# A gated delta-rule layer with expert routing on one core: later convolutions behind each inverse, and the inverse's first blocks stored and loaded first

## The reference

```
x = hidden_states                                   # (1, 2048, 512)
h = layernorm(x)
q, k, v = (silu(conv4(h @ W)) for W in (Wq, Wk, Wv))   # causal convolution over 4 tokens, per column
q, k = l2norm(q), l2norm(k);  beta = sigmoid(h @ Wb)
for each token t:                                   # per head, state S is 64 x 64
    u = beta * (v - k @ S);  S = S + outer(k, u);  o = (q / 8) @ S
x = x + (rmsnorm(o) * norm_w) @ Wo
```

## Time and profile before

| | us |
|---|---|
| median of 3 runs (lowest, highest) | 1327.56 (1323.68, 1330.0) |
| the profiled execution | 1325.61 |
| its span, first to last instruction | 1323.6 |
| PE busy | 1274.0 |
| DVE busy | 865.5 |
| ACT busy | 373.7 |
| POOL busy | 338.3 |
| mean granted TensorE clock | 0.988 |

### The profile page before, as it was taken

One profiled execution on the slowest core, in us unless ns is written; L12 is line 12 of the kernel. 1 busy time (PEld: TensorE's weight loads), 2 busy tenths in 40 slices (PEclk: granted clock), 3 DMA queues, 4 the chain that ended last, 5 costly groups with the idle time before them and its releaser, 6 DMA issues.

```text
span 1323.6 us, 27812 instructions
## 1 busy us (share of the span) xinstructions
PE 1274.0 (96%) x8725; PEld 794.4 (60%) x8726; DVE 865.5 (65%) x2411; ACT 373.7 (28%) x818; POOL 338.3 (26%) x398
## 2 busy tenths in 40 slices
PE   8978999998998999999999999999999999999997
PEld 7857777876776565444444555555555555555553
DVE  4896697669669325545111577777777777777774
ACT  5745554655453323120000011111111111111111
POOL 1211224322233122114643012122222212122212
PEclk9989999999998999999999999999999999999999
DMA  5524842743563594565456556666666565664420
GB/s 161 98 42 103 129 113 73 156 112 77 110 143 117 141 226 113 124 234 202 178 204 235 129 128 135 132 137 137 137 139 136 128 137 131 131 138 71 73 50 9
DMA packets 208516, 171.08 MB, mean 129 GB/s; under 512 B 71473, under 2 KB 160561, under 8 KB 208433
## 3 DMA queue, kind: packets, MB, share of 16 engines
q1 hardware_dynamic: 135056, 114.16, 33.8%
q0 software_dynamic: 16496, 34.23, 13.1%
q10 hardware_dynamic: 56880, 21.54, 7.8%
HBM read 91.06 MB, written 82.73 MB: 131 GB/s over the span
## 4 chain that ended last, share of the span: by engine, by line
PE 54%; DVE 2%; issue 0%; DMA 0%; POOLq 0%; ACT 0%; DVEq 0%
PE pD L2260 15%; PE pG L2235 14%; PE pU L2244 14%; PE pG L2192 3%; PE pU L2192 3%; PE pD L2211 3%; PE pU L2186 1%; PE pD L2206 0%; DVE ups L2133 0%; DMA out<-y,ix 0%; POOLq L1949 0%; DVE w L1833 0%; DVE w L1834 0%; DVE route_keep L1832 0%; DVE qf L1845 0%
## 5 line engine op out<-in xcount | busy, mean ns | idle before, releaser
L2133 DVE STREAM_TRANSPOSE ups<-a 32x96 f32<-32x96 f32 (+1 forms) x1248 | 326.2, 261 | 42.3
L2025 POOL DMA_INDIRECT out<-y,ix x79 | 123.0, 1557 | 477.1 <-ACT y L2086 322.5
L2260 PE MATMUL pD<-w,ups 128*128 (+1 forms) x474 | 216.6, 592 | 0.7 <-DVE ups L2133 0.7
L2244 PE MATMUL pU<-w,xsT 128*128 x632 | 199.9, 459 | 0.0
L2235 PE MATMUL pG<-w,xsT 128*128 x632 | 199.9, 458 | 0.0
L2235 PEld LDWEIGHTS pG<-w,xsT 128*128 128x128 f32 x632 | 119.5, 189 | 88.4 <-issue 37.6
L2244 PEld LDWEIGHTS pU<-w,xsT 128*128 128x128 f32 x632 | 120.1, 190 | 66.9
L955 PE MATMUL pProj<-front_region 128*128 128x256 f32 x624 | 154.0, 390 | 2.2 <-ACT front_region L698 1.6
L2260 PEld LDWEIGHTS pD<-w,ups 128*128 128x128 f32 (+1 forms) x474 | 90.0, 190 | 93.2 <-issue 76.8
L1358 DVE SCALAR_TENSOR_TENSOR front_region<-front_region,cw 128x256 f32<-128x256 f32 x288 | 133.7, 505 | 9.4 <-ACT front_region L734 5.8
L955 PEld LDWEIGHTS pProj<-front_region 128*128 128x128 f32 x624 | 112.9, 190 | 19.7 <-ACT front_region L734 2.2
(11 more groups left out here) (253 smaller groups left out, 1612.4 us busy)
## 6 DMA issues: line engine op xcount, KB each, us to landing
w<-in_up_T SPq DMA_DIRECT2D x16, 1408.0 KB
slot_rows<-zeros SPq DMA_DIRECT2D x79, 266.0 KB, 6.9
xs<-slot_rows ACTq DMA_DIRECT2D x316, 64.0 KB
w<-in_down_T SPq DMA_DIRECT2D x16, 512.0 KB
front_region<-in_L_attn_hidden_states SPq DMA_DIRECT2D x16, 256.0 KB, 3.3
x2r<-in_L_attn_hidden_states SPq DMA_DIRECT2D x16, 256.0 KB, 4.5
partial_sums<-x2r SPq DMA_DIRECT2D x16, 256.0 KB, 3.7
x_normed<-x2n SPq DMA_DIRECT2D x16, 256.0 KB, 2.2
```

The lines of the kernel that those rows point to most:

```text
L2025: pool.indirect_dma_start(out=flat, out_offset=bass.IndirectOffsetOnAxis(ap=ix[1 - par][:, 0:1], axis=0), in_=y[1 - par][:, :], in_offset= ...
L2133: dve.transpose(aT[par][B * to:B * to + B, 0:n, rows], a[rows, 0:len(IC) * P].rearrange("p (c n) -> p c n", c=len(IC))[:, 0:n, B * to:B * ...
L2244: mm = pe.matmul(pU[0][:, 0:I], xsT[par][:, k, :], w[:, bass.ds(slot, 1), 2 * I * k + I:2 * I * (k + 1)], start=(k == 0), stop=(k == DC - 1))
L2260: mm = pe.matmul((pYlast if end(q) else pYq)[:, :], aT[1 - par][0:m, c, :], down[0:m, :, UPW + D * c:UPW + D * (c + 1)], start=(c == 0), s ...
```

## The change

A list of pairs, `LATE` = (2, 4, 6), names those whose projections finish in the odd units -1, 3 and 7. For them:

- DVE does one `conv` in the odd unit (projections 4 and 5, slot 4) and three in the even unit behind it (6 to 11, in slots 0 to 2). The next pair's first `conv` moves from slot 2 to slot 3. ACT's silus follow, and two accumulators more are allocated (a ring of eight).
- Values are turned ahead of queries: PE has vT, vT, qT, qT in slots 2 to 5, DVE `make_v` in slots 3 and 4 and `q_sums` in slot 5 and slot 0 of the next unit, ACT `q_squares` in slots 4 and 5. The waits on `pT0` follow.
- POOL's `halo` of values and queries and `q_coefs` move to later slots.

For all inverses: the two stores get semaphores of their own (`s_vf`, `s_tf`) and SP waits for the first only before it loads. The pieces are loaded in the order 1, 3, 0, 2. The lower two get a semaphore of their own (`s_tl`), and `merge_w` waits for these two alone; `merge_x` waits for the other four. Before the first piece of `NP` of a tile that opens a group, SP waits for the second store.

```diff
-KQ_RING, KT_RING, VH_RING, NP_RING, TT_RING, ACC_RING = 4, 7, 5, 6, 4, 6
+KQ_RING, KT_RING, VH_RING, NP_RING, TT_RING, ACC_RING, ACC_MORE = 4, 7, 5, 6, 4, 6, 2
+LATE = (2, 4, 6)
+    acc = acc + [sb(f"acc_more{i}", [P, PW])[:, :] for i in range(ACC_MORE)]
...
# SP
-                sp.dma_start(td_d[b][0:4 * H, :], LT[0:4 * H, :]).then_inc(s_vf, 16)
+                sp.dma_start(td_d[b][0:4 * H, :], LT[0:4 * H, :]).then_inc(s_tf, 16)
-                for b in range(4):
+                for b in (1, 3, 0, 2):
...
-                                 vd_d[t // 4][lanes, :].rearrange("g (j i) -> j g i", i=HB)).then_inc(s_tt[t % TT_RING], 16)
+                                 vd_d[t // 4][lanes, :].rearrange("g (j i) -> j g i", i=HB))\
+                        .then_inc((s_tt if b % 2 == 0 else s_tl)[t % TT_RING], 16)
+                    if b == 0 and t % 4 == 0:
+                        sp.wait_ge(s_tf, 16 * (t // 4 + 1))
...
-                            sp.wait_ge(s_vf, 32 * ((u + 1) // 4 + 1))
+                            sp.wait_ge(s_vf, 16 * ((u + 1) // 4 + 1))
...
# POOL
+                    if even and (u + 4) // 2 in LATE and s == 1:
+                        halo((u + 6) // 2, 1)
-                    if s == 2 and even and pair_ok((u + 6) // 2) and u + 6 > 2:
+                    if s == (3 if (u + 4) // 2 in LATE else 2) and even and pair_ok((u + 6) // 2) and u + 6 > 2:
                         halo((u + 6) // 2, 2)
...
# ACT
-                least(act, s_silu, g - ACC_RING + 1)
+                least(act, s_silu, g - len(acc) + 1)
...
+                    if even and old in LATE and s in (1, 2, 3):
+                        silu(3 * DC * old + 4 + 2 * s)
+                        silu(3 * DC * old + 5 + 2 * s)
...
-                    if even and s in (3, 5) and pair_ok(pk):
+                    if even and s in ((4, 5) if old in LATE else (3, 5)) and pair_ok(pk):
                         for g in range(2):
-                            silu(3 * DC * pk + s - 3 + g)
+                            silu(3 * DC * pk + (0 if s < 5 else 2) + g)
...
-                    if even and s in (2, 3) and pair_ok(old) and 1 < old < PAIRS - 1:
-                        q_squares(2 * old + s - 2)
+                    if even and s in ((4, 5) if old in LATE else (2, 3)) and pair_ok(old) and 1 < old < PAIRS - 1:
+                        q_squares(2 * old + s % 2)
...
# PE
+                    if p - 1 in LATE:
+                        pe.wait_ge(s_qsq, 2 * p)              # kT
+                if p in LATE and t % 2 == 0:
+                    pe.wait_ge(s_vh, t + 2)                   # qT
...
-                pe.wait_ge(s_tt[t % TT_RING], 96 * (t // TT_RING + 1))
+                pe.wait_ge(s_tl[t % TT_RING], 32 * (t // TT_RING + 1))     # merge_w
+                pe.wait_ge(s_tt[t % TT_RING], 64 * (t // TT_RING + 1))     # merge_x
...
-                            qT(2 * old)
+                            (vT_turn if old in LATE else qT)(2 * old)      # slot 2, and so on
...
# DVE
-                        if s == 0 and old < PAIRS - 1:
+                        if s == 0 and old < PAIRS - 1 and old not in LATE:
                             conv(3 * DC * old + 10)
-                        if s in (3, 4) and 0 < old < PAIRS - 1:
+                        if s < 3 and old in LATE:
+                            conv(3 * DC * old + 6 + 2 * s)
+                        if s in (3, 4) and old in LATE:
+                            make_v(2 * old + s - 3)
+                        if s == 5 and old in LATE:
+                            q_sums(2 * old)
+                        if s in (3, 4) and 0 < old < PAIRS - 1 and old not in LATE:
                             q_sums(2 * old + s - 3)
...
-                    if even and pair_ok(pk) and s in (2, 4):
-                        conv(g0 + s - 2)
+                    if even and pair_ok(pk) and s in ((3, 4) if old in LATE else (2, 4)):
+                        conv(g0 + (2 if s == 4 else 0))
...
-                        if s in (0, 2, 4):
+                        if s in (0, 2, 4) and pq not in LATE:
                             conv(g0 + 4 + s)
+                        if s == 4 and pq in LATE:
+                            conv(g0 + 4)
```

More of the change, by code:

```diff
@@ L282, in attention @@
     s_tt = [sem(f"inverse_loaded{i}") for i in range(TT_RING)]
+    s_tl = [sem(f"inverse_lower_loaded{i}") for i in range(TT_RING)]
+    s_tf = sem("inverse_first_rows_stored")
     s_w3 = [sem(f"proj_w_loaded{i}") for i in range(3)]
@@ L682, in _ @@
                         halo((u + 7) // 2, 0)
-                        halo((u + 7) // 2, 1)
+                        if (u + 5) // 2 not in LATE:
+                            halo((u + 7) // 2, 1)
         @block.scalar
@@ L745, in silu @@
                     out = kq[p % KQ_RING][:, i % DC + (DC if i >= 2 * DC else 0), :]
-                act.activation(out, acc[g % ACC_RING], ACT.Silu).then_inc(s_silu, 1)
+                act.activation(out, acc[g % len(acc)], ACT.Silu).then_inc(s_silu, 1)
             def k_rows(t):
@@ L875, in _ @@
                         q_squares(opening(u, s) - 18)
-                    if even and s == (4 if old == PAIRS - 1 else 1) and pair_ok(old):
+                    if even and old in LATE and s in (1, 2, 3):
+                        silu(3 * DC * old + 4 + 2 * s)
+                        silu(3 * DC * old + 5 + 2 * s)
+                    if even and s == (4 if old == PAIRS - 1 else 1) and pair_ok(old) and old not in LATE:
                         silu(3 * DC * old + 10)
@@ L992, in vT_turn @@
                     pe.wait_ge(s_ksq, NT)
+                elif t % 2 == 0 and t // 2 in LATE:
+                    pe.wait_ge(s_silu, place(t // 2, 2 * DC - 1) + 1)
+                    pe.wait_ge(s_th, t // 2 + 2)
+                    pe.wait_ge(s_ksq, t + 2)
                 elif t % 2 == 0:
@@ L1301, in _ @@
                         if even and pair_ok(old) and 0 < old < PAIRS - 1:
-                            qT(2 * old + 1)
+                            (vT_turn if old in LATE else qT)(2 * old + 1)
                         if even and old == PAIRS - 1:
@@ L1310, in _ @@
                         if even and pair_ok(old) and 0 < old < PAIRS - 1:
-                            vT_turn(2 * old)
+                            (qT if old in LATE else vT_turn)(2 * old)
                         if not even and pair_ok(new) and new != 1:
@@ L1319, in _ @@
                         if even and pair_ok(old) and 0 < old < PAIRS - 1:
-                            vT_turn(2 * old + 1)
+                            (qT if old in LATE else vT_turn)(2 * old + 1)
                         if even and old == PAIRS - 1:
@@ L1357, in conv @@
                         at = DC * (1, 2, 0)[i // DC] + i % DC
-                        ins = dve.scalar_tensor_tensor(out=acc[(g + h) % ACC_RING], in0=raw[:, at, j:j + PW],
-                                                       scalar=cw[:, at, j:j + 1], in1=acc[(g + h) % ACC_RING],
+                        ins = dve.scalar_tensor_tensor(out=acc[(g + h) % len(acc)], in0=raw[:, at, j:j + PW],
+                                                       scalar=cw[:, at, j:j + 1], in1=acc[(g + h) % len(acc)],
                                                        op0=ALU.mult, op1=ALU.add)
@@ L1648, in _ @@
                             inverse(NT // 4 - 1, 4)
-                        if s == (4 if old == 1 else 5) and 0 < old < PAIRS - 1:
+                        if s == (4 if old == 1 else 5) and 0 < old < PAIRS - 1 and old not in LATE:
                             make_v(2 * old)
@@ L1652, in _ @@
                             make_v(3)
-                    if not even and s == 0 and pair_ok((u + 3) // 2) and 2 < u + 3 < NT - 2:
+                    if not even and s == 0 and pair_ok((u + 3) // 2) and 2 < u + 3 < NT - 2 and (u + 3) // 2 not in LATE:
                         make_v(2 * ((u + 3) // 2) + 1)
+                    if not even and s == 0 and (u + 3) // 2 in LATE:
+                        q_sums(2 * ((u + 3) // 2) + 1)
                     if u + 3 == NT - 2 and s in (1, 2):
```

22 lines of the change are left out of this document (15 added, 7 removed).

## The result

| | before | after |
|---|---|---|
| median, first comparison (6 runs each) | 1327.53 us | 1316.97 us (1312.83 to 1321.43) |
| ratio, 95% interval | | 0.9913 [0.9891, 0.9935] |
| median, second comparison (17 and 4 runs) | 1328.75 us | 1314.43 us (1312.69 to 1321.25) |
| ratio, 95% interval | | 0.9879 [0.9853, 0.9905] |
| the profiled execution, its span | 1325.61, 1323.6 us | 1320.15, 1318.4 us |

The change makes the kernel faster by about 0.9 to 1.2%: the medians differ by 10.6 us in the first comparison and by 14.3 in the second. The ratio is an estimate of its own and not the quotient of the two medians; its interval is 8.6 to 14.5 us in the first comparison and 12.6 to 19.5 in the second. The forecast was 1315, with a range of 1309 to 1325.

What follows compares the result with a forecast made beforehand. PE, busy 1274.0 of 1323.6 us, was taken as the bound. Waits of 8.62 us plus 2.82 of clock, 11.4 us, took the profiled 1325.61 to 1314.2; the forecast was placed at 1315, range 1309 to 1325.

Steps and rivals of the forecast that it cites:

- The four waits: PE's waits at unit -1's Gram matmul, hop_u of units 3 and 7, and merge_w of tile 12 go: 8.62 us.
- Unit 3: 2.48 + 1.41 = 3.89 us: PE's 2.48 us wait at hop_u behind the second residual goes, and the half clock following it gives back 1.41.
- Unit 7: 2.50 us: PE's wait at hop_u behind the second residual goes: 2.50 us, with no clock term.
- Unit -1: 2.60 + 1.41 us: PE's 2.60 us wait at tile 4's Gram matmul behind the score mask goes, plus 1.41 of half clock after it.
- `merge_w` of tile 12: 1.04 us: PE's wait for the DMA loading the inverse goes, with one store awaited and the two needed blocks loaded first: 1.04 us.
- The inverse ends "some 6 us earlier": Unit 3's inverse, ending at 214.81 us, ends some 6 us earlier while PE reaches its merge_w only about 4 us earlier.
- Units 0, 4 and 8 at no cost: The added convolution, 2.70 to 3.49 us, fits into 4.64 us of DVE idle time ahead of unit 4's second residual: cost 0.
- VectorE beside GpSimd: The convolution moved to slot 1 beside POOL's rescaling costs DVE 0.79 us more per unit, covered by idle time.
- The clock rival: The clock gives nothing back in the low stretches after the waits; only 8.62 us go, 1318 us; chance 0.15.
- DVE the bound: With no cover left in units 0, 4 and 8, two added convolutions each cost 6.98 us; some 1336 us; chance 0.06.
- doesn't do what it says: DVE stays late for units 3 and 7's residuals, or waits reappear elsewhere; about 5 us gained, 1322 us; chance 0.26.
- The signs of being wrong: PE waiting for DVE or ACT in units 0, 4, 8; equal waits elsewhere in units 3, 7; low clock in new places.

Runs made afterwards that it cites:

- each half, taken alone: Against the kernel before: only the new order and semaphores of stores and loads, 1325.05 us, ratio 0.9972; only the late convolutions, 1318.7 us, ratio 0.9932.
- Pair 2 alone: The changed kernel with LATE = (2,), so that only pair 2 is late; 1321.94 us in one execution.
- the loads alone: The changed kernel with no pair late and six accumulators, keeping only the new order and semaphores of stores and loads; 1325.05 us, ratio 0.9972.
- the four multiplications: The changed kernel plus four chained 128x1024 multiplications on DVE in slot 1 of units 0, 4 and 8, ahead of o_sums; 1325.99 us in one execution.
- the early keys: The changed kernel with pair 2's convolution of keys 2 and 3 moved from slot 4 to slot 3 of unit -2; ratio 0.9914.

## Why the prediction was right, point by point

- **The four waits.** Right in place and number. All are absent in both profiles of the change, and each half, taken alone, removes its own and leaves the others.
- **Unit 3: 2.48 + 1.41 = 3.89 us.** Measured 31.7 to 27.6 and 27.4, so 4.1 to 4.3. Pair 2 alone splits it: 1.6 us clock, the rest the wait and a little more.
- **Unit 7: 2.50 us.** Measured 3.1, mostly the wait; a wait of 0.38 us for the normed output (POOL, L639) that unit 7 had in the profile of before is absent in the change as well.
- **Unit -1: 2.60 + 1.41 us.** Right in kind, too large in size: 3.1 us over the stage. The wait was not a fixed 2.60 us but what was left between DVE's fixed end and PE's arrival, which moves with the clock (2.60, 1.62, 1.24 us). And of the 1.41 us of clock only 0.5 is left between the two profiles of the record (37.95 - 34.87 - 2.60), as an earlier low stretch came to lie over more of PE's work.
- **`merge_w` of tile 12: 1.04 us.** The wait goes. In the change its loads began 1.96 us after the issue of the first store, in the profile of before 2.59 us after it, so one store less in the wait gave 0.6 us, where the prediction took 0.42 from the earlier trace rows. That store is not always so quick: in unit 11 it took 3.0 to 4.1 us in six of the eleven profiles with the new order, and `merge_w` waited 0.13 us at most. The time of the loads alone moved by more than the wait; that is the open part.
- **The inverse ends "some 6 us earlier".** Mis-sized: against the start of its unit it ended 4.7 us earlier (22.7 to 18.0 us). The two convolutions took 6.37 us, but with them gone DVE waited 1.41 us for PE ahead of the logits. It did not matter, as no `merge_w` waits for it.
- **Units 0, 4 and 8 at no cost.** Right: 24.3, 28.5 and 28.5 us before and after. The chain through `q_sums` and the x2 sum, costed at 0 with 3 x 1.0 as its other end, cost nothing there either: PE waits for no x2 sum in these units. In unit 6, where no pair is late, that wait grew from 0.72 to 1.09 us. The reading of the cover was too simple. I added up the idle time ahead of the second residual and got 4.64 us. The logits copy and `make_v` in the same queue go late sooner, as the four multiplications showed. Had a second convolution been added ahead of them, the wait would have come at a place that the prediction did not name.
- **VectorE beside GpSimd.** The moved convolution took 3.50 us beside POOL's rescaling, as the 3.49 of the earlier trace rows let expect, and the idle time ahead of the second residual covered it. The Trainium skill ("GPSIMD Engine Reference", Key points) says that a VectorE instruction with two SBUF inputs contends with GpSimd, and this trace agrees (3.50 against 2.69 us).
- **The clock rival.** The likeliest case gave back two stretches of clock; in truth one of them is there in three runs of four and one is part of a stage that shifts. With 1.6 us in three profiles of four and the 0.5 us of unit -1, this term was worth 1 to 2 us and not 2.82, and what made up for it in the sum was unit 11 (2.1 us for 1.04) and unit 7 (3.1 for 2.50). That the total came out so near is in part luck. The same wait of 2.48 us was followed by clock 0.50 three times and by 1.00 once. The Trainium skill ("TensorE: Matmul & The Clock Gate", Part 1) has the observing window run freely, and these four profiles fit it.
- **DVE the bound, doesn't do what it says.** Neither came. Both did come where they were provoked: four extra multiplications made DVE the bound in units 0, 4 and 8, and in unit -1 the early keys turned a wait of 5.65 us into one of 5.54 elsewhere.
- **The signs of being wrong.** One of them is there by its words: the low clock turned up in two places where it wasn't, behind the first wait for the input (20.3 to 23.7 us) and in unit 13 (470.9 to 474.3). The loads alone, with no pair late, show the first as well, so the moved convolutions are not needed for it. The wait goes back to a later load of the input in the one case, and to nothing that the profile shows in the other, so neither speaks against the four waits.

## What to carry to other kernels

Before a wait for an engine's queue is costed as a gain, find what ends the queue. In units 3 and 7 the work that left was work that nothing there needed, and the wait vanished; in unit -1 putting the keys first only moved it. When work is moved into a gap, check every instruction behind it in that queue for its own reader, not only the one in front of which the idle time is listed. And compare stage by stage from a common event: here a longer wait for the input at 20 us and a wait in unit 13 hid half of the gain from a comparison of two spans.

## What the runs showed of the hardware that I had not expected

- The low clock of units 10 and 11 did not end when PE was busy again. After the change it was 0.50 for 13.7 us, 406.0 to 419.7, with PE busy 12.70 of them; in the earlier trace rows it is 10.2 us with 9.51 busy. All fourteen profiles have such a stretch there, 10.2 us or longer. Why, the runs do not show.
- A convolution on DVE slows down beside some of POOL's work and not beside all of it. In the kernel before it took 3.49 us at 232.90, with a POOL instruction of 128x512 over part of it (233.04 to 234.28), and 2.71 us at 104.12, with one of 128x16 over nearly all of it (103.72 to 106.64).
- In unit 13 PE stood still for 1.70 us in the middle of four matmuls, with nothing released that the profile shows, and the clock fell behind it; the unit took 28.0 us for 24.4. Waits of this kind, 0.6 to 3.2 us long, appear in that place in eight of the eleven profiles with the new order of loads and in none of the three with the old one. SP issues the loads of the shared expert's input there, and the DMA share is 1.01 in the stretch of 470.90. A busy DMA by itself is not enough: at the same place in the kernel before, 476 to 479 us, it is 1.07, and PE does not stop. Whether the order has a part in it or it is chance with eleven and three, the runs do not settle. If it has, the change would gain more without it, 3.6 us in this profile and 4.9 in its second.
